# The attention stage and its output projection in one block, softmax sums inverted once per row, v projections between the first scores

## The reference

```
attention 0:  q, k, v = x Wq + bq, x Wk + bk, x Wv + bv        (per head)
              y = softmax(q k^T / 4 + causal mask) v ;  y Wo + bo
mixture 0:    8 experts, top 2 of a router, and a gated shared expert of 512
attention 1:  q, k with rotary embedding, no mask, no biases ;  y Wo^T
mixture 1:    4 experts of 1024, each takes its 256 best tokens
```

## Time and profile before

| | us |
|---|---|
| median of 3 runs | 821.68 |
| profiled execution | 823.66 |
| its span | 821.8 |
| mean granted clock of TensorE | 0.851 of full |
| PE busy, DVE busy | 668.9 (81%), 565.9 (69%) |
| first score matmul, attention 0 and 1 | 34.03, 398.35 |
| first transposed scores | 70.63, 441.10 |
| end of the last product with v | 198.6, 612.4 |
| first projected tile added to x | 221.28, 629.57 |

### The profile page before, as it was taken

How to read it: one execution, slowest core, us unless ns; L and a number is a source line. 1 busy time by engine, 2 the same in 40 slices (tenths; PEclk the granted TensorE clock), 3 DMA queues, 4 the chain that set the end, 5 groups by cost and what they waited for, 6 DMA issues and landing times. The chain is left out here.

```text
span 821.8 us, 13473 instructions
## 1 busy us (share of the span) xinstructions
PE 668.9 (81%) x5096; PEld 452.5 (55%) x5096; DVE 565.9 (69%) x1071; ACT 359.4 (44%) x687; POOL 197.8 (24%) x297
## 2 busy tenths in 40 slices
PE   3759899996379999859899999999974549879776
PEld 3525455553357888747544444444433318768666
DVE  4336788890657767655545999999917688889545
ACT  3103676673125444412103888888861323353240
POOL 4301455544312212212200111111122040242220
PEclk9855999995589999969755999999996657999899
DMA  5930234310031111014700222222001120111001
GB/s 187 260 124 19 74 93 97 84 51 33 14 121 39 38 57 39 1 51 179 205 0 1 63 65 64 66 65 67 27 26 64 46 103 1 52 59 69 29 1 51
DMA packets 19481, 55.24 MB, mean 67 GB/s; under 512 B 6368, under 2 KB 7648, under 8 KB 18016
## 3 DMA queue, kind: packets, MB, share of 16 engines
q1 hardware_dynamic: 15840, 46.08, 18.4%
q0 software_dynamic: 3584, 8.39, 3.3%
HBM read 36.37 MB, written 17.83 MB: 66 GB/s over the span
## 5 line engine op out<-in xcount | busy, mean ns | idle before, releaser
L383 ACT ACTIVATE probs<-ps 128x512 f32<-128x512 f32 x448 | 213.3, 561 | 104.9 <-PE ps L316 104.5
L301 PE MATMUL ps<-k_stack,q_stack 62*128 62x512 f32 x448 | 179.9, 477 | 18.0 <-DVE row_max L481 12.7
L484 DVE TENSOR_REDUCE row_max<-ps 128x1 f32<-128x1024 f32 x128 | 150.9, 1216 | 33.2 <-PE ps L301 33.1
L316 PE MATMUL ps<-q_stack,k_stack 64*128 64x512 f32 x448 | 163.7, 445 | 10.4 <-ACT probs L383 6.6
L316 PEld LDWEIGHTS ps<-q_stack,k_stack 64*128 64x128 f32 x448 | 78.4, 195 | 87.1 <-ACT probs L383 65.0
L331 PE MATMUL ps<-probs,v_ones 128*32 128x256 f32 (+7 forms) x2048 | 122.0, 358 | 3.8 <-POOL probs L432 3.0
L481 DVE CUSTOM_DVE_ANT_0 part_rows<-ps,wide_mask 128x1024 f32<-128x1024 f32 (+7 forms) x128 | 92.0, 756 | 42.2 <-PE ps L301 25.4
L301 PEld LDWEIGHTS ps<-k_stack,q_stack 62*128 62x128 f32 x448 | 81.6, 205 | 49.1 <-DVE row_max L481 21.4
L331 PEld LDWEIGHTS ps<-probs,v_ones 128*32 128x32 f32 x2048 | 53.3, 114 | 49.3 <-issue 17.3
L1067 POOL TENSOR_TENSOR w_l_m<-y_sums,w_h_m 128x2048 fp32r<-128x2048 f32 x8 | 36.7, 4589 | 119.2 <-ACT w_h_m L1074 119.2
L432 POOL TENSOR_SCALAR_AFFINE_SELECT probs<-probs 128x128 f32<-128x128 f32 x128 | 37.1, 295 | 98.9 <-ACT probs L383 97.5
(11 more groups left out here) (188 smaller groups left out, 1321.4 us busy)
## 6 DMA issues: line engine op xcount, KB each, us to landing
y_sums<-in_w_experts SPq DMA_DIRECT2D x8, 1024.0 KB, 4.9
q_parts<-part_rows SPq DMA_DIRECT2D x12, 512.0 KB, 4.5
k_parts<-part_rows SPq DMA_DIRECT2D x12, 512.0 KB, 4.3
q_stack<-q_parts SPq DMA_DIRECT2D x32, 192.0 KB, 3.2
k_stack<-k_parts SPq DMA_DIRECT2D x32, 192.0 KB, 3.9
y_sums<-in_w_chunks SPq DMA_DIRECT2D x12, 384.0 KB, 3.0
head_sums<-sums POOLq DMA_DIRECT2D x32, 128.0 KB, 2.0
y_sums<-head_sums POOLq DMA_DIRECT2D x64, 64.0 KB, 2.5
```

The lines of the kernel that those rows point to most:

```text
L301: mm = pe.matmul(scores_bank(s, a, b), stack("q_stack", h, slice(0, TOP))[:, qt * P:(qt + 1) * P], stack("k_stack", h, slice(0, TOP))[:, a ...
L316: pe.matmul(bank(at % 3, 0, b - a), stack("k_stack", h, slice(0, SIDE))[:, kt * P:(kt + 1) * P], stack("q_stack", h, slice(0, SIDE))[:, a: ...
L383: act.activation(probs[:, t % 4, a:b], bank(at % 3, 0, b - a), ACT.Exp).then_inc(exp_done, 1)
L484: dve.tensor_reduce(row_max[:, h % 2, qt:qt + 1], scores_bank(s, 0, end), AX.X, ALU.max).then_inc(scores_free, 1)
```

## The change

Attention and output projection become one block. What each part does:

- The low parts of the q/k units are made by VectorE in layer 0 (POOL did them); POOL adds `bias_o` to x at the start of attention 0.
- The eight units follow each other. In both layers the v projection of token tile n stands behind score tiles 2n and 2n+1 of heads 0 and 1, in PSUM banks 0 and 1; the keep-warm matmuls there are gone. In layer 0, VectorE takes v out between its maxima.
- `masked_scores` is other memory (`y_sums`), and VectorE's wait for the writes of units 4 to 7 is gone. ScalarE and SP still wait for them.
- Sums are written a second time to DRAM, one row per head (`sum_rows`). Groups of heads 0-7 and 8-13 are read packed (64 columns), inverted by VectorE, written back and spread over 16 rows each by SP. `load_sums` loads y alone.
- Heads 14 and 15 never go through DRAM: `own_head` shuffles, inverts, multiplies and splits on VectorE, and SP and ScalarE store the parts into `yt_h` and `yt_l` by 4 + 4 transfers a head.
- The projection is split: the half of heads 0-7 for all tiles, six keep-warm matmuls, the half of heads 8-15. The last two heads of attention 0 get one keep-warm matmul of 256 columns per key tile.
- The memset of `wide_mask` stands earlier in `load_and_split`.

```
-WARM = (1, 3)
+GROUPS = ((0, H // 2), (H // 2, H - 2))
...
-        masked_scores = part_rows[:, 0:2, :].bitcast(F32)
+        masked_scores = mem["y_sums"][:, 1, :, :]
...
+            def store_heads(queue, h, transfers, signal, count): ...
...
+                if h == 9:
+                    read_group(0)
+                if h == 11:
+                    write_group(0)
+                if h == 12:
+                    spread_group(0)
+            read_group(1)
+            write_group(1)
+            spread_group(1)
+            store_heads(sp, H - 2, range(2 * QUADS), own_step, 4)
+            store_heads(sp, H - 1, range(QUADS), own_step, 9)
             sp.wait_ge(extra_in, 16)
-            for k in range(KD):
-                sp.wait_ge(stored[k], 32 * H // KD)
+            sp.wait_ge(group_low, 2)
...
-            for u in range(4):
+            for u in range(8):
                 unit(u)
-            for t in range(NT):
-                project_v(t)
-            for u in range(4, 8):
-                unit(u)
-            pe.wait_ge(v_out, NT)
             pe.wait_ge(unit_out, 8)
             for s in range(2 * NT):
                 scores(s, 0)
                 scores(s, 1)
-                for _ in range(WARM[layer]):
-                    keep_warm()
+                if s % 2:
+                    project_v(s // 2)
+            pe.wait_ge(v_out, NT)
...
+                if causal and t + 2 * NT == H * NT:
+                    pe.wait_ge(scores_free, H * NT)
+                if causal and t + 2 * NT >= H * NT:
+                    keep_warm(3, D)
...
+            pe.wait_ge(group_low, 1)
+            pe.wait_ge(scores_free, H * NT)
+            for t in range(NT):
+                project_out(t, 0)
+            for _ in range(6):
+                keep_warm(0, HALF)
+            pe.wait_ge(group_low, 2)
+            pe.wait_ge(own_stored, 2 * 16 * 2 * QUADS)
+            for t in range(NT):
+                project_out(t, 1).then_inc(o_ready, 1)
...
+                pool.dma_start(dram["sum_rows"][h].rearrange("(c x) -> c x", c=QUADS), sums[HD:P:2 * HD, h % 2, :]
+                               ).then_inc(sums_written, 16)
...
-            if causal:
-                dve.wait_ge(written[2], 48)
-                dve.wait_ge(written[3], 48)
+            group(0, slice(0, P))
+            invert_group(1)
+            dve.wait_ge(sums_out, H - 1)
+            own_head(H - 2, sums[:, (H - 2) % 2, :])
+            group(1, slice(0, P - 2 * HD))
+            dve.wait_ge(pv_ready, H)
+            own_head(H - 1, bank(7, (H - 1) % 2 * (T // QUADS), T // QUADS))
```

More of the change, by code:

```diff
@@ L125, in _ @@
             dve.memset(mem["v_ones"][:, :, :, HD:2 * HD], 1.0).then_inc(preset, 1)
+            dve.memset(mem["wide_mask"][:, 0:T - P], 0.0).then_inc(preset, 1)
             dve.memset(mem["eps"][:, :], EPS).then_inc(preset, 1)
@@ L372, in _ @@
                                ).then_inc(high_ready, 1)
[L373 to L377, removed]
+            if rope:
+                for tile in range(NT):
+                    act.wait_ge(v_ready, tile + 1)
+                    act.activation(v_ones[:, :, tile, 0:HD], bank(tile % 2, 0, D).rearrange("p (h d) -> p h d", d=HD),
+                                   ACT.Copy).then_inc(v_out, 1)
             def exps(t):
@@ L397, in _ @@
                     take_sums(t // NT - 1)
-            take_sums(H - 1)
+            store_heads(act, H - 1, range(QUADS, 2 * QUADS), own_step, 9)
+            norm.scalar(act)
         @block.gpsimd
@@ L498, in finish_max, with unit_low, invert_group @@
                 dve.transpose(max_rows[:, h % 2, :], mem["max_parts"][:, :].bitcast(F32)).then_inc(max_ready, 1)
-            for u in range(4):
+            def unit_low(u):
+                g, n = u // 2, u % 2
+                high, low = [parts[:, g % 2, l, n * HALF:(n + 1) * HALF] for l in range(2)]
+                dve.wait_ge(high_ready, u + 1)
+                if g >= 2:
+                    dve.wait_ge(written[g - 2], 48)
+                dve.tensor_tensor(low, flat[:, u % 2, :], high.bitcast(F32), ALU.subtract).then_inc(low_ready, 1)
+            for u in range(8):
                 unit_to_flat(u)
+                if not rope and u:
+                    unit_low(u - 1)
             if not rope:
-                for t in range(NT):
-                    v_to_sbuf(t)
-            for u in range(4, 8):
-                unit_to_flat(u)
-            if causal:
-                dve.wait_ge(written[2], 48)
-                dve.wait_ge(written[3], 48)
+                unit_low(7)
+            def invert_group(g):
+                rows = slice(0, T * (GROUPS[g][1] - GROUPS[g][0]) // 64)
+                dve.wait_ge(group_in[g], 16)
+                dve.reciprocal(shared_sums[rows, :], shared_sums[rows, :]).then_inc(group_done, 1)
             for h in range(H):
@@ new lines, in _ @@
+            group(0, slice(0, P))
[5 more added lines that the diff above has]
+            own_head(H - 1, bank(7, (H - 1) % 2 * (T // QUADS), T // QUADS))
+            dve.wait_ge(extra_in, 16)
+            if not rope:
+                dve.wait_ge(biased, NT)
+            for t in range(NT):
+                dve.wait_ge(o_ready, t // 2 * 2 + 2)
+                dve.tensor_tensor(mem["x"][:, t, :], out_bank(t), mem["x"][:, t, :], ALU.add).then_inc(o_out, 1)
+                dve.wait_ge(o_out, t + 1)
+                norm.statistics(dve, t)
@@ L519, in norm_statistics @@
+            norm.vector(dve)
 def norm_statistics(dve, stats, mv, rows, t, step, count):
```

221 lines of the change are left out of this document (107 added, 114 removed).

## The result

The changed kernel took 773.18, 777.16, 778.56 and 776.99 us, median **777.08**, beside 821.88 for the kernel before on the same chip: ratio 0.946 (95% interval 0.942 to 0.950), 45 us less. A second time, on another chip, it took 775.33 (ratio 0.939, 0.934 to 0.944). The forecast was 769, with 748 to 785 as range. The profiled execution is the one of 773.18 us, the fastest of the four, its span 771.4; against 823.66 of the one before that is 50.5 less, where the prediction's sum said 52.5. On the chip of both_edits, bias_late, no_end_warm and v_by_two, two of seven executions of the kernel before (829.09 and 1844.79 us) were in a slow state and are in no ratio.

A forecast was written before the change was run, and what follows sets the result against it. TensorE at 1.2 GHz was taken to bound the score stages, with near-idle ends besides; 12.7 + 19.9 + 12.7 + 7.2 = 52.5 us off 823.66 gives 771.2, less 2.0 to the median: 769, range 748 to 785.

The forecast's parts named there:

- Stage of attention 0: Scores of heads 0 and 1 in attention 0 run from 34.0 to 57.9 instead of to 70.63: -12.7 us.
- two small edits at the start: Start of attention 0: moved memset gains up to 0.8 us, low parts on VectorE lose up to 1.5; together zero.
- score-to-score switch of 0.15: Score stages: a second score tile in a row with new weights costs TensorE 0.15 us, between 0 and 0.30.
- Stage of attention 1: Scores of heads 0 and 1 in attention 1 start at 391.3 and end at 421.2 instead of 441.10: -19.9 us.
- I take neither: Attention 0's last two heads: 16 keep-warm matmuls add 3 us if the clock falls, none if they hold it; neither counted.
- Ends: From last v product to first projected tile: -12.7 us in attention 0, -7.2 in attention 1.
- bound of -2: End of attention 0: gain of only 2 us if all five DMA hops take the longest landing, 4.2 us.
- Loops, nothing: Steady loops of both attentions: compute left alone, POOL's changed writes and loads cost or gain nothing.
- stays the same length: Behind attention 1's end: the per-tile addition and statistics keep their length, so no change.
- (a): Rival, score stages: clock rises and VectorE sets them, 14.5 us less, 755 us in all; chance 0.20.
- (b): Rival, ends: DMA round trips cost their longest, -2 instead of -12.7 and 3 lost in attention 1, 783 us; chance 0.15.
- (c): Rival, loops: they stay at 1.2 GHz after the new stages, 86 us lost against 52.5, 855 us; chance 0.05.

The follow-up runs named there:

- both_edits: Changed kernel with all v projections ahead of the first score and no keep-warm in attention 0's last two heads: 756.59 us, ratio 0.920 to the kernel before.
- bias_late: both_edits with POOL's eight bias additions moved from the start of attention 0 to behind its loop: 758.06 us, ratio 0.924 to the kernel before.
- no_end_warm: both_edits without the six keep-warm matmuls that fill the wait for the last head's stores, in both attentions: 756.55 us, ratio 0.919 to the kernel before.
- v_by_two: Changed kernel with two v projections after every fourth score tile instead of one after every second: 777.09 us, ratio 0.942 to the kernel before.
- changed_again: The changed kernel unedited, run a second time beside v_at_units on one chip: 775.33 us, ratio 0.939 to the kernel before.
- no_tail_warm: Changed kernel without the 16 keep-warm matmuls in the last two heads of attention 0: 768.58 us, ratio 0.929 to the kernel before.
- scratch_apart: Kernel before with only VectorE's scratch for masked scores in other memory and its wait for the k_parts writes gone: 810.76 us, ratio 0.982.
- v_at_units: Changed kernel with the v projections put back between the fourth and fifth q/k unit: 763.81 us, ratio 0.926 to the kernel before.
- v_first: Changed kernel with all v projections after the last q/k unit and ahead of the first score, both attentions: 760.41 us, ratio 0.922 to the kernel before.
- best_again: The kernel of bias_late unedited, run a second time beside v_at_units: 758.97 us, ratio 0.920 to the kernel before.

## Why the prediction came out right, and where it did not

The mechanism held at the places that carried the sum: the score stages at 1.2 GHz set by TensorE's columns, VectorE's wait on its scratch, the stack load that is late next in attention 1, DMA round trips hidden behind the last heads. Of its sum of 52.5 us, 50.4 are in the traces. By its steps:

- **Stage of attention 0**, -12.7: -12.8. The two small edits at the start came out at 0.55 later together, taken as zero (in changed_again at nothing, 33.99). The score-to-score switch of 0.15 was 0, and a wait of 0.5 for VectorE's last copy of v, which the sum left out, took a part of that back: the agreement to 0.1 is in part luck. The same is true in attention 1, where the switch explains 1.2 of the 2.0 more that were gained; the rest is the first pair at full clock (1.3), less the wait for ScalarE's last copy (0.5).
- **Stage of attention 1**, -19.9: -21.9. The load at 363.11 plus 4.5 gave the start, as worked out.
- **"I take neither"** for the keep-warm of the last two heads of attention 0: this is the term that was wrong. The clock fell as it had before, and the price was not 16 x 0.213 = 3.4 but 7.6 on TensorE, because each adds a switch at the same 0.30 that the prediction used a paragraph above. 6.1 us of it show in the trace, 5.9 against no_tail_warm; the rest fell into waits that TensorE had there anyway (0.8 ahead of the last product with v).
- **Ends**, -12.7 and -7.2: -13.9 and -8.5, both inside their bounds. The last head took 3.5 as said; stores and products took 5.2 instead of 6.5. (The bound of -2 doesn't follow from its own terms: five hops at 4.2 instead of 2.3 are 9.5, which leaves -3.2.)
- **Loops, nothing**: -3.3 in attention 0. It need not be the change: the earlier trace rows's 7.1 us a head held, but the profiled execution before had dips of the clock in that loop, and scratch_apart, whose loop is the same code, runs from the first transposed to the last scores in 101.1 us where the trace of before took 106.2. The prediction read one head as steady and didn't read the clock over the whole loop.
- **Behind attention 1, "stays the same length"**: +2.6. This is no scatter: from the first addition to the end, all ten traces with the joined end take 194.0 to 196.7 us and the three without it 191.2 to 192.8. Counted from the first addition, VectorE's instructions start 1.4 to 1.7 us earlier than in the kernel before from 22 to 87 us, and 2.1 later from 123 us on, after stretches at the low clock in mixture 1 (0.66 from 650 to 660). It isn't the six keep-warm matmuls (no_end_warm has 196.7). Why the joined end moves the clock there stays open.
- **From the sum to 769**: the profiled execution before lay 2 over the median, the one after 4 under it. That is 6 of the 8 us by which the forecast was low; no step of the sum stands for it.

Of the rivals, (a) didn't come in the changed kernel or any other of the eleven: the stages stay at 0.50 but for their first microseconds (at most 4.8; v_at_units, the highest in attention 0, has 0.66 over its stage) and, in v_by_two alone, two stretches of 3.4 us in each. "TensorE: Matmul & The Clock Gate", Part 1, of the Trainium skill would have had them at full clock; the measurement decides against it here, also where v products alternate with scores. (b) is excluded by the 8.8 us; (c) by a clock of 0.94 to 1.00 from 10 us into each loop on, up to the last two heads of attention 0.

What the prediction did not ask is what the title's edit does against the simplest alternative. It compared the v projections with the keep-warm matmuls that they replaced. Its own model, 5.12 + 2.4 us a head for v in a stage where VectorE needs 7.1, against idle TensorE before the first score, says that they belong ahead of it; v_first and v_at_units measured that at 9.5 us in attention 0 alone (8.9 against changed_again). Why the clock stays low in these stages, with TensorE busy throughout, no run shows.

## What to carry to other kernels

Filler that is replaced by useful work at the bound engine looks like a gain; price the useful work against an idle place, not against the filler. Before giving a keep-warm instruction a price, look at what the clock did there so far, and count its switch. And when an engine's operation is moved off a critical start, see whose work it lands beside: POOL's additions cost VectorE as much at the new place (1.0 us) as at the old one, and changed which transfer came first besides.

## What the hardware showed that I had not expected

- VectorE beside POOL: with both working out of SBUF, a cast of 256 columns takes 0.84 to 0.85 us instead of 0.29, a subtraction of 512 columns 1.07 to 1.21 instead of 0.68; POOL's eight additions take 6.8 to 7.0 instead of the 5.47 of the earlier trace rows. "SBUF — State Buffer", "Who interferes with whom", of the Trainium skill says that VectorE and GpSimd share one pair of ports, that a cast can take the pair with a lock, and that an operation with two SBUF inputs contends with GpSimd's reads; these rows agree, and VectorE's reads of PSUM (0.75 us for 512 columns beside POOL and alone) were not slowed.
- A change between products of 62 rows of weights and of 128 rows costs 0.30 us at 1.2 GHz, from one 62-row product to the next nothing. Whether the rows or another difference of the two kinds sets it was not separated.
- Dips of the clock inside a steady, full loop are in one trace and not in another of the same code: 5.1 us between before and scratch_apart (106.2 and 101.1), 3.6 between no_end_warm and both_edits.
- A store of 16 KB that was issued behind a large weight load landed after 3.2 and 3.5 us (bias_late, best_again), ahead of it after 1.9 (both_edits).
